# A four-layer graph and expert model on one core: the turn of the expert results, the grouping of the relational stage, and constant matmuls on TensorE

## The chip, the cores and the metric

The kernel runs on one core of one Trainium2 chip. A core has a matrix engine (TensorE, PE in the profile), a vector engine (VectorE, DVE), an activation engine (ScalarE, ACT), a general engine (GpSimd, POOL) and an engine that here only issues transfers (SyncE, SP). Each takes its instructions in the order in which they are written and waits on semaphores that the others raise. The metric is the time of one execution in microseconds on the device. Lower is better.

## What is computed

8192 rows of 128 numbers go through four layers, each added to its input:

```python
x = x + _L0_gnn_ref(_layernorm(x, axis=-1), adj, ...)       # gated graph layer, 3 rounds
x = x + _L0_ffn_ref(_layernorm(x, axis=-1), ...)            # 8 experts, top 2, relu
x = x + _L1_gnn_ref(_layernorm(x, axis=-1), nodemask, adj, ...)   # relational graph layer
x = x + _L1_ffn_ref(_layernorm(x, axis=-1), ...)            # 8 experts, top 2, gelu
```

An expert layer scores each row against 8 experts, takes the best two, and adds their weighted results:

```python
h = gelu(einsum('end,edh->enh', xe, W1) + b1)      # hidden 512; relu in the first expert layer
y = einsum('enh,ehd->end', h, W2) + b2
out = (weights[:, :, None] * sel).sum(axis=1)      # the two chosen experts of each row
```

The relational layer multiplies the rows by a weight, gates them with a sigmoid, and sums them over the neighbours that the adjacency names. A branch for general adjacencies is in the kernel; with the inputs at hand it isn't taken.

## The kernel before, in words

The program has four stages one behind the other, and each ends with results in DRAM that the next one reads: the gated graph layer (to about 470 us), experts 1 (to 806), the relational layer (to 1058), experts 2 (to 1388), and a short last stage that adds the results and stores them. Names that begin with e1 and e2 belong to the expert stages, those with c to the relational stage.

**Experts.** The rows come sorted by expert, in 36 blocks of 512 (NBLK; GT = 4 tiles of 128 rows each). The last 12 blocks consist of two halves of 256 with an expert each. Buffers go round in rings of three (RING), PSUM banks in pairs. A function `rounds` runs `step(b, ...)` on each engine: blocks 0 to 2 written out, 3 to 20 in a loop on the device, 21 to 35 written out. The hidden width of 512 is cut into four pieces, c = 0 to 3 (CH). Each matmul product runs as three passes (lines 205 to 207), since operands are split in a high and a low part of 16 bits.

- PE, in step b, does for each c `up_c(b+1, c)` and `down_c(b, c)`, and behind the four of them `turn(b-1)`: four transposes (line 1547) of the block's results, which wait for `collect(b-1)`.
- ACT, for each c, does `hidden` (line 1586: bias and activation out of PSUM into e1hf) and `hi` (line 1592: the high part into e1hs), with `hi(c)` one place behind `hidden(c+1)`.
- DVE, in step b, does `collect(b-1)` (line 1630: scale and bias of the results into e1yT), in every third step `addresses` (lines 1617 to 1623: where the rows of three blocks go, and with which weight), `share_out(b-2)` (line 1639: the transposed results times their weights into e1ys), and the four `lo(b+1, c)` (line 1605: the low parts into e1hs).
- SP loads the rows of a block transposed (`load`) and their tags (`read_tags`).
- POOL sends each block's e1ys in four indirect transfers to its rows in `results` (line 1511).

**Relational stage.** 16 groups of 512 rows run through 21 steps as a software pipeline; line by line, an engine's step s works on groups s, s-1, s-2 and s-4 at once. On PE: `turn_a` (transposes of the normalised rows c_tok_a, line 1861), `turn_b` (transposes of the rows for the next expert layer, line 1925), `scores` (their eight scores each), `values` (lines 1877 and 205 to 207: four tiles q, in two PSUM banks v), and `neighbours` (line 1890: the sums by adjacency). ACT copies the transposes out of PSUM (`turned_a`, c_xT_a; `turned_b`, c_xT_b). DVE turns scores into S (line 2141) and picks the two best experts for a batch of groups; BATCHES says which. POOL sends rows to their places in `slots` for experts 2 at a rate that `relational_sends` sets for each step. PE's bank TA holds the transposes of turn_a, TBk those of turn_b, RL the sums of neighbours.

## Time and profile before

| | |
|---|---|
| median of three runs | 1425.64 us (1419.89 to 1427.88) |
| profiled execution | 1428.36 us |
| its span | 1426.6 us |
| mean granted TensorE clock | 0.787 |
| PE busy | 918.1 us, 64% |
| DVE busy | 905.9 us, 64% |
| ACT busy | 765.8 us, 54% |
| POOL busy | 733.9 us, 51% |

The profile is of one execution. Its span is what lies between the first and the last recorded instruction; the execution's own time is 1.8 us longer. A share of busy time is a mean over stages that differ, so it has to be read by stage. In the lists an instruction has its start, its duration, its engine and line, what it writes and reads, and in brackets how long the engine stood idle before it and what ended that. Matmuls overlap: one is listed with 0.38 us while the next starts 0.22 us later. The clock stands as a share of full speed, so 0.50 is 1.2 GHz and 1.00 is 2.4 GHz.

### The profile page before, as it was taken

To read this page: it belongs to the slowest core of one execution; us is meant where nothing else is said; L and a number is where in the kernel's file an instruction comes from. 1 tells how busy PE (TensorE), PEld (TensorE's weight loads), DVE (VectorE), ACT (ScalarE), POOL (GpSimd) and SP (SyncE) were. 2 spreads that over 40 slices of the span, in tenths; PEclk is the share of its full clock that TensorE was granted. 3 is DMA by queue.
4 is the path that set the end of the run, shared out by engine and by line. 5 is a ranking of instruction groups with operands and counts; after the bars stand their busy time and mean duration, and the time that the engine had idled before them with its cause. 6 is when DMAs were issued, how large, how long until landed. Compare 5 with 4: busy or idle time off the path is not lost. (4 is left out here: it accounts for less than half of the span.)

```text
span 1426.6 us, 23103 instructions
## 1 busy us (share of the span) xinstructions
PE 918.1 (64%) x5850; PEld 519.1 (36%) x5851; DVE 905.9 (64%) x2456; ACT 765.8 (54%) x1392; POOL 733.9 (51%) x717
## 2 busy tenths in 40 slices
PE   2368778888862357888787176656432968888820
PEld 1244344444432123434565133323210433346620
DVE  5967799999985345555544367767642645554626
ACT  2476767677762145666565165656431655666710
POOL 3501132876757646556544416567566444655540
PEclk9579999999995679899988555555556998999955
DMA  9233221221201524424221223321131342333209
GB/s 249 90 127 94 77 46 23 59 61 48 59 22 42 136 58 100 91 67 85 64 50 45 71 90 119 104 65 55 32 62 52 87 105 58 84 67 70 61 28 340
DMA packets 199164, 115.62 MB, mean 81 GB/s; under 512 B 155084, under 2 KB 175710, under 8 KB 198528
## 3 DMA queue, kind: packets, MB, share of 16 engines
q1 hardware_dynamic: 169008, 69.54, 20.8%
q0 software_dynamic: 17408, 34.13, 7.4%
q10 hardware_dynamic: 12624, 10.49, 2.8%
q8 instruction: 54, 0.88, 0.3%
q14 instruction: 70, 0.57, 0.1%
HBM read 43.80 MB, written 51.61 MB: 67 GB/s over the span
## 5 line engine op out<-in xcount | busy, mean ns | idle before, releaser
L644 POOL DMA_INDIRECT slots<-ROWS,pos x256 | 265.4, 1037 | 78.5 <-issue 71.4
L1511 POOL DMA_INDIRECT results<-e1ys,e1home x144 | 155.5, 1080 | 136.1 <-DVE e1ys L1639 93.7
L1511 POOL DMA_INDIRECT results<-e2ys,e2home x144 | 151.1, 1049 | 136.2 <-DVE e2ys L1639 93.0
L1586 ACT ACTIVATE e1hf<-psum,VT 128x512 f32<-128x512 f32 (+1 forms) x192 | 104.3, 583 | 151.6 <-PE psum L207 82.0
L1605 DVE SCALAR_TENSOR_TENSOR e1hs<-e1hf,e1hs 128x512 f16<-128x512 f32 x144 | 95.6, 690 | 127.4 <-ACT e1hs L1592 88.9
L1586 ACT ACTIVATE e2hf<-psum,VT 128x512 f32<-128x512 f32 (+1 forms) x192 | 104.8, 582 | 126.0 <-remote 59.1
L1605 DVE SCALAR_TENSOR_TENSOR e2hs<-e2hf,e2hs 128x512 f16<-128x512 f32 x144 | 95.8, 691 | 112.5 <-ACT e2hs L1592 83.0
L1363 POOL TENSOR_TENSOR a_Z<-a_Z,a_H 128x512 f32<-128x512 f32 x48 | 68.2, 1420 | 161.5 <-ACT a_Z L1093 159.2
L205 PE MATMUL psum<-e2hs,W 128*128 128x512 f16 (+1 forms) x192 | 66.7, 347 | 55.9 <-DVE e2hs L1605 25.9
L205 PE MATMUL psum<-a_hT,WHH 128*128 128x512 f16 x144 | 58.8, 408 | 52.5 <-ACT a_Z L1093 48.3
L205 PE MATMUL psum<-e1xT,W 128*128 128x512 f16 (+1 forms) x192 | 67.6, 352 | 38.5 <-DMA e1xT<-slots 16.7
L205 PE MATMUL psum<-e1hs,W 128*128 128x512 f16 (+1 forms) x192 | 67.4, 351 | 35.8 <-DVE e1hs L1605 24.9
L1592 ACT ACTIVATE e1hs<-e1hf 128x512 f16<-128x512 f32 x144 | 86.9, 631 | 0.0
L1592 ACT ACTIVATE e2hs<-e2hf 128x512 f16<-128x512 f32 x144 | 86.7, 631 | 0.0
L205 PE MATMUL psum<-e2xT,W 128*128 128x512 f16 (+1 forms) x192 | 66.7, 348 | 23.4 <-issue 11.0
L1804 POOL TENSOR_TENSOR c_rs<-c_var,mhalf 128x12 f32<-128x12 f32 (+2 forms) x22 | 40.5, 1843 | 79.9 <-DVE c_var L2082 45.1
L207 PE MATMUL psum<-e1xT,W 128*128 128x512 f16 (+1 forms) x192 | 67.7, 353 | 3.3 <-issue 3.2
L206 PE MATMUL psum<-e1hs,W 128*128 128x512 f16 (+1 forms) x192 | 67.5, 352 | 2.7 <-issue 1.7
L206 PE MATMUL psum<-e1xT,W 128*128 128x512 f16 (+1 forms) x192 | 67.5, 351 | 2.7 <-issue 2.7
L207 PE MATMUL psum<-e1hs,W 128*128 128x512 f16 (+1 forms) x192 | 67.4, 351 | 2.7 <-issue 2.5
L207 PE MATMUL psum<-e2xT,W 128*128 128x512 f16 (+1 forms) x192 | 66.5, 346 | 1.6 <-issue 1.5
L206 PE MATMUL psum<-e2xT,W 128*128 128x512 f16 (+1 forms) x192 | 66.5, 346 | 0.4 <-issue 0.4
(363 smaller groups left out, 2643.6 us busy)
## 6 DMA issues: line engine op xcount, KB each, us to landing
c_G<-results SPq DMA_DIRECT2D x32, 256.0 KB
d_G<-results SPq DMA_DIRECT2D x32, 256.0 KB, 5.2
slots<-slots SPq DMA_DIRECT2D x16, 264.0 KB
W<-in_L_ffn_W_dram SPq DMA_DIRECT2D x16, 256.0 KB, 3.4
kept<-a_cut SPq DMA_DIRECT2D x16, 256.0 KB, 2.6
slots<-ROWS,pos POOLq DMA_INDIRECT x256
W<-kept SPq DMA_DIRECT2D x8, 512.0 KB
out_dram<-X ACTq DMA_DIRECT2D x16, 256.0 KB, 7.1
```

The costliest lines, as they stand in the source:

```text
L205: pe.matmul(out, lhs(0), rhs(0), start=start, stop=False, skip_group_check=True)
L206: pe.matmul(out, lhs(0), rhs(1), start=False, stop=False, skip_group_check=True)
L207: return pe.matmul(out, lhs(1), rhs(0), start=False, stop=stop, skip_group_check=True)
L644: pool.indirect_dma_start(out=slots, out_offset=bass.IndirectOffsetOnAxis(ap=k["pos"][:, c, t:t + 1], axis=0), in_=k["ROWS32"][:, t, :], i ...
L1363: pool.tensor_tensor(Z[p % 2][:, :], Z[p % 2][:, :], H[p][:, :], ALU.mult).then_inc(zh_sb, 1)
L1511: pool.indirect_dma_start(out=k["results"][m], out_offset=bass.IndirectOffsetOnAxis(ap=home[:, GT * b + q:GT * b + q + 1], axis=0), in_=ys ...
L1586: t = act.activation(hf[c][:, cols], HB[c][:, cols], func, bias=VT[:, bass.ds(e * CH + b1_col + c, 1)], scale=1 / PS)
L1592: act.activation(hs[j][:, 0, c, :], hf[c][:, :], ACT.Copy, scale=AS).then_inc(h_hi, 1)
L1605: dve.scalar_tensor_tensor(out=hs[j][:, 1, c, :], in0=hf[c][:, :], scalar=AS, in1=hs[j][:, 0, c, :], op0=ALU.mult, op1=ALU.subtract).then_ ...
L1804: pool.tensor_tensor(rstd[s % 4][:, lo:hi], var[s % 2][:, lo:hi], k["mhalf"][:, lo:hi], ALU.pow)\
```

## The change

In the expert stages, `turn(b-1)` on PE goes from the end of step b to the place behind `down_c(b, 1)`. On DVE the step shares out block b-1, not b-2, behind `lo(b+1, 1)`; behind the loop only the last block is left to share. `addresses` comes in the second step of three, not the third, and SP reads a block's tags ahead of the next load.

In the relational stage the first two groups form one batch of the selection, so there are 8 batches and not 9, and `relational_sends` starts a step later, with 8. PE does `values` in two halves, the first (v = 0) ahead of `scores`. ACT does `turned_b` ahead of `norms_a` in the first steps. And `stir` multiplies the identity by a constant tile of weights, 256 columns, into banks that are written again before they are read: 40 times at the start, and in each of the 21 steps 6 times ahead of `turn_a`, 5 ahead of `turn_b` and 8 ahead of `neighbours`. Nothing reads these products.

```diff
@@ experts, SP @@
+                if 1 <= b and b + 2 < NBLK:
+                    read_tags(b + 2, rows.pop(b + 2))
                 if b + RING == EARLY:
...
                 if b + RING < NBLK:
                     sp.wait_ge(h_ps, 4 * b + 4)
                     rows[b + RING] = load(b + RING)
-                if 1 <= b and b + 2 < NBLK:
-                    read_tags(b + 2, rows.pop(b + 2))
@@ experts, PE: within the loop over c, and behind it @@
-                if not isinstance(b, int) or b:
-                    turn(b - 1, 1 - v)
+                    if c == 1 and (not isinstance(b, int) or b):
+                        turn(b - 1, 1 - v)
@@ experts, DVE @@
                     collect(b - 1, 1 - v)
-                if j == RING - 1:
+                if j == 1:
                     addresses(b - j, i)
-                if not isinstance(b, int) or b > 1:
-                    share_out(b - 2, (j - 2) % RING, i - (j < 2), v)
                 for c in range(CH):
                     if not last(b):
                         lo(b + 1, (j + 1) % RING, c)
+                    if c == 1 and (not isinstance(b, int) or b):
+                        share_out(b - 1, (j - 1) % RING, i - (j < 1), 1 - v)
...
             collect(end, end % 2)
-            for b in (end - 1, end):
-                share_out(b, b % RING, b // RING, b % 2)
+            share_out(end, end % RING, end // RING, end % 2)
@@ relational stage @@
-BATCHES = [(0, 1), (1, 1)] + [(g, 2) for g in range(2, 16, 2)]
+BATCHES = [(g, 2) for g in range(0, 16, 2)]
...
-    first = ROUTED + 1
+    first = ROUTED + 2
-    wanted = [0 if s < first else (8, 6, 2)[s - first] if s < first + 3 else 8 if s < NG else CARRY for s in range(n)]
+    wanted = [0 if s < first else 8 if s < NG else CARRY for s in range(n)]
...
-            def values(g, p):
+            def values(g, p, v):
                 pe.wait_ge(a_sb, g + 1)
-                for q in range(GT):
-                    v = q // 2
+                for q in range(2 * v, 2 * v + 2):
...
+            def stir(bank, n):
+
+                for i in range(n):
+                    pe.matmul(bank[:, 0:256], ident[:, :], k["WREL"][:, 0, 0, :], start=True, stop=True,
+                              skip_group_check=True)
+
+            stir(TA, 40)
+
             def step(s):
+                stir(TA, 6)
                 if 0 <= s - 1 < NG:
                     turn_a(s - 1, (s - 1) % 2)
+                stir(TBk, 5)
                 if 0 <= s - 4 < NG:
                     turn_b(s - 4)
+                if 0 <= s - 1 < NG:
+                    values(s - 1, (s - 1) % 2, 0)
                 if 0 <= s - 4 < NG:
                     scores(s - 4)
                 if 0 <= s - 1 < NG:
-                    values(s - 1, (s - 1) % 2)
+                    values(s - 1, (s - 1) % 2, 1)
                 if 0 <= s - 2 < NG:
+                    wait_from(pe, rel_sb, s - 3)
+                    stir(RL[s % 2], 8)
                     neighbours(s - 2, s % 2)
@@ relational stage, ACT @@
                     turned_a(s - 1, (s - 1) % 2)
+                if 0 <= s - 4 < NG:
+                    turned_b(s - 4)
                 if s < SPLIT:
                     norms_a(s, s % 2)
-                if 0 <= s - 4 < NG:
-                    turned_b(s - 4)
```

How this stands in the engines' rows is shown at three places. On PE, in step 2 of experts 1, the four transposes of turn (identf and e1yT into PSUM) change place; one piece of the difference, with the part between left out by the list itself (the matmuls of up 2, down 2, up 3 and down 3):

```order
@@ -1388,4 +1388,5 @@
 L1450 TENSOR_LOAD owner
 L1450 ISA x2
+L1547 MATMUL psum<-identf,e1yT 128x128 x4
 L205 ISA
 L205 MATMUL psum<-e1xT,W 128x512
@@ -1408,5 +1409,4 @@
 L207 REGISTER_ALU
 L207 MATMUL psum<-e1hs,W 128x512
-L1547 MATMUL psum<-identf,e1yT 128x128 x4
 L1426 UNCONDITIONAL_BRANCH
 L1426 ISA
```

The turn moved ahead of the second half of the step's matmuls. On DVE, steps 1 and 2 of experts 1, before (e1hs is lo, e1yT collect, the four e1chosen to e1share are addresses, e1ys is share_out):

```order
L1605 SCALAR_TENSOR_TENSOR e1hs<-e1hf,e1hs 128x512 x4
L1450 TENSOR_LOAD owner
L1450 ISA x2
L1630 ISA
L1630 TENSOR_SCALAR e1yT<-psum,VT 128x512
L1617 TENSOR_TENSOR e1chosen<-e1label,owned 128x12
L1619 TENSOR_TENSOR e1part<-e1chosen,e1label 128x12
L1620 SCALAR_TENSOR_TENSOR e1home<-e1chosen,e1label 128x12
L1623 TENSOR_TENSOR e1share<-e1part,e1label 128x12
L1639 TENSOR_TENSOR e1ys<-psum,e1share 128x512
L1605 SCALAR_TENSOR_TENSOR e1hs<-e1hf,e1hs 128x512 x4
```

and after, the end of step 1 and step 2:

```order
L1605 SCALAR_TENSOR_TENSOR e1hs<-e1hf,e1hs 128x512 x2
L1639 TENSOR_TENSOR e1ys<-psum,e1share 128x512
L1605 SCALAR_TENSOR_TENSOR e1hs<-e1hf,e1hs 128x512 x2
L1450 TENSOR_LOAD owner
L1450 ISA x2
L1630 ISA
L1630 TENSOR_SCALAR e1yT<-psum,VT 128x512
L1605 SCALAR_TENSOR_TENSOR e1hs<-e1hf,e1hs 128x512 x2
L1639 TENSOR_TENSOR e1ys<-psum,e1share 128x512
L1605 SCALAR_TENSOR_TENSOR e1hs<-e1hf,e1hs 128x512 x2
```

The share of a block now follows its own collect, with two of the four lo ahead of it and two behind, where it stood behind the collect of the block after it. On PE in a step of the relational stage, before, the scores (WGATE) stand right behind the transposes of turn_a and turn_b:

```order
L1861 MATMUL psum<-ident,c_tok_a 128x128 x8
L1925 MATMUL psum<-ident,ROWS 128x128 x8
L205 MATMUL psum<-WGATE,c_xT_b 128x8
L206 MATMUL psum<-WGATE,c_xT_b 128x8
L207 MATMUL psum<-WGATE,c_xT_b 128x8
```

and after, with the first half of values (relbias, WREL and c_xT_a) and five matmuls of stir (WREL and ident):

```order
L1860 MATMUL psum<-ident,c_tok_a 128x128 x8
L1938 MATMUL psum<-WREL,ident 128x256 x5
L1923 MATMUL psum<-ident,ROWS 128x128 x8
L1875 MATMUL psum<-relbias,ones 128x256 x2
L205 MATMUL psum<-WREL,c_xT_a 128x256
L206 MATMUL psum<-WREL,c_xT_a 128x256
L207 MATMUL psum<-WREL,c_xT_a 128x256
L1875 MATMUL psum<-relbias,ones 128x256 x2
L205 MATMUL psum<-WREL,c_xT_a 128x256
L206 MATMUL psum<-WREL,c_xT_a 128x256
L207 MATMUL psum<-WREL,c_xT_a 128x256
L205 MATMUL psum<-WGATE,c_xT_b 128x8
```

The ten matmuls of the first two q of values moved ahead of the scores, and the matmuls of stir are new.

## Rows read from the trace of the kernel before

**Rows 1.** By stage: length, busy time (instructions) by engine, PEclk, DMA share, GB/s.

```profile
500.00:791.00 291.00, 225.36 (x1254) 128.33 (x1254) 152.18 (x273) 167.87 (x325) 154.88 (x144) 0.88 0.32 69
...
806.00:1058.00 252.00, 138.92 (x985) 76.45 (x985) 169.83 (x783) 132.64 (x274) 142.17 (x157) 0.51 0.25 78
...
1100.00:1373.00 273.00, 220.33 (x1255) 127.25 (x1252) 147.81 (x270) 167.05 (x323) 141.28 (x134) 0.91 0.32 71
```

**Rows 2.** Timeline, PE, experts 2: start, us, engine, line, out<-in, count.

```profile
1135.61 0.38 PE L207 MATMUL psum<-e2xT,W 128*128 128x512 f16 x1
...
1139.29 0.38 PE L207 MATMUL psum<-e2hs,W 128*128 128x512 f16 x1
...
1141.23 0.38 PE L207 MATMUL psum<-e2xT,W 128*128 128x512 f16 x1
...
1142.09 0.60 PE L1547 MATMUL psum<-identf,e2yT 128*128 128x128 f32 x4
```

**Rows 3.** The same stretch on ACT and DVE.

```profile
1136.71 1.14 ACT L1592 ACTIVATE e2hs<-e2hf 128x512 f16<-128x512 f32 x2
...
1138.79 0.75 DVE L1630 TENSOR_SCALAR e2yT<-psum,VT 128x512 f32<-128x512 f32 x1
```

**Rows 4.** Timeline, half blocks of experts 1, PE and DVE.

```profile
770.13 0.42 PE L207 MATMUL psum<-e1xT,W 128*128 128x256 f16 x1
...
774.18 0.88 DVE L1630 TENSOR_SCALAR e1yT<-psum,VT 128x256 f32<-128x256 f32 x2 [0.81 <-issue]
```

**Rows 5.** Timeline, first and last of the 66 steps counted, PE and DVE.

```profile
530.97 0.38 PE L207 MATMUL psum<-e1hs,W 128*128 128x512 f16 x1
...
534.85 0.75 DVE L1630 TENSOR_SCALAR e1yT<-psum,VT 128x512 f32<-128x512 f32 x1
...
1364.73 0.42 PE L207 MATMUL psum<-e2hs,W 128*128 128x256 f16 x1
...
1367.82 0.88 DVE L1630 TENSOR_SCALAR e2yT<-psum,VT 128x256 f32<-128x256 f32 x2 [0.69 <-issue]
```

**Rows 6.** Timeline, POOL, ends of both expert stages.

```profile
789.11 0.98 POOL L1511 DMA_INDIRECT results<-e1ys,e1home  x1 [7.76 <-DVE e1ys L1639]
...
803.28 0.98 POOL L1511 DMA_INDIRECT results<-e1ys,e1home  x1 [0.30 <-issue]
...
1370.80 0.98 POOL L1511 DMA_INDIRECT results<-e2ys,e2home  x1 [7.49 <-DVE e2ys L1639]
```

**Rows 7.** Relational stage, one step: ACT, PE; then DVE grouped by line.

```profile
885.75 1.02 ACT L1993 ACTIVATE c_xT_a<-psum 128x1024 f16<-128x1024 f16 x1 [0.96 <-PE psum L1861]
887.99 1.02 ACT L2006 ACTIVATE c_xT_b<-psum 128x1024 f16<-128x1024 f16 x1 [1.22 <-remote]
...
889.07 0.19 PE L205 MATMUL psum<-WGATE,c_xT_b 128*128 128x8 f16 x1 [3.42 <-ACT c_xT_b L2006]
...
889.49 0.60 PE L1877 MATMUL psum<-relbias,ones 1*128 1x256 f16 x2
...
892.06 0.60 PE L1877 MATMUL psum<-relbias,ones 1*128 1x256 f16 x2
...
L2141 DVE TENSOR_TENSOR S<-psum,c_rs 128x32 f32<-128x32 f32 x16 | 3.0, 188 | 21.7 <-PE psum L207 21.7
```

**Rows 8.** Relational stage: windows with the clock, and PE in them.

```profile
996.80:999.70 2.90, 2.81 (x27) 2.52 (x24) 1.92 (x7) 1.50 (x5) 2.29 (x3) 0.50 0.18 60
999.70:1003.40 3.70, 1.24 (x18) 0.78 (x19) 1.75 (x12) 2.41 (x3) 3.08 (x4) 0.96 0.13 42
1003.40:1007.00 3.60, 3.60 (x15) 1.10 (x14) 2.57 (x13) 0.00 (x0) 3.10 (x3) 0.50 0.08 28
...
1002.99 0.27 PE L206 MATMUL psum<-WREL,c_xT_a 128*128 128x256 f16 x1
1003.10 0.27 PE L207 MATMUL psum<-WREL,c_xT_a 128*128 128x256 f16 x1
```

**Rows 9.** Relational stage, DVE by line: an operation of the selection.

```profile
L582 DVE TENSOR_TENSOR v_wide<-S,v_top 128x64 f32<-128x64 f32 (+1 forms) x9 | 2.0, 221 | 0.3
```

## The prediction

> **What bounds the kernel now.** I read the table of busy time by stage first [rows 1], then the order of time on each engine inside one step. In the two expert stages TensorE (PE) is the bound: 225.36 of 291 us and 220.33 of 273 us busy, at a granted clock of 0.88 and 0.91, while DVE is busy for about half of the time. The relational stage is another matter: at a clock of 0.51 (the 1.2 GHz level) PE is busy for 139 of 252 us and DVE for 170, so there waits between engines set the pace.
>
> A step of an expert stage that runs without a pause is on PE an unbroken row of 24 matmuls and 4 transposes [rows 2]: the last matmul of up_c(b+1, 3) starts at 1135.61 and again at 1141.23, a period of 5.62 us. The transposes of turn(b-1) stand last in the step (1142.09). Beside it runs the chain that I take for the main thing in this change [rows 3]: after up_c of c=3, at 1135.61, ACT does hidden(3) and two hi (1136.71 to 1137.85), DVE two lo and collect, which ends at 1138.79 + 0.75 = 1139.54. That is 3.93 us after the start of the matmul that released it. No engine waits for collect now: the turn that needs it comes 2.55 us later.
>
> **Experts, the turn.** The change puts turn(b-1) right behind the matmuls of down_c(b, 1), whose last starts at 1139.29; the next could start at 1139.51. So even in a smooth step collect's end and the slot of the turn meet within 0.03 us. This has a consequence: turn, up_c(b+1, 2), down_c(b, 2) and up_c(b+1, 3) then all stand behind collect(b-1), and collect(b) stands behind up_c(b+1, 3). The loop closes: 3.93 (chain) + about 0.1 (PE starts on a signal) + 0.44 (turn: 0.60 for its four transposes, less the 0.16 by which the next matmul starts before the end of the last) + 0.65 + 0.65 (up 2, down 2) + 0.43 (up 3 to its last start) = 6.20 us, against the 5.62 that PE's own work takes. That is +0.58 us for a smooth step. The half blocks at the end have a longer chain (770.13 to 774.18 + 0.88, 4.93 us [rows 4]), so their loop is about 7.2 us.
>
> Most steps aren't smooth: 33 steps of experts 1 lie 7.8 us apart on average, of experts 2 7.6; 11 and 10 of the periods are under 5.75. For each step b = 3 to 35 of both stages I took the lateness: collect's end less the slot behind the last matmul of down_c(b, 1) (its start + 0.22). The first is 535.60 - 531.19 = 4.41 us, and the last 1368.70 - 1364.95 = 3.75 [rows 5]. Over 33 steps the positive ones add up to 52.8 us in experts 1 (31 of 33 are late) and 47.2 in experts 2 (29 of 33). The smooth steps hold 6.4 and 3.8 of it, the steps with a pause 46.3 and 43.4. Their true price lies between nothing (PE waits again later in such a step anyway, and the new wait only takes that one's place) and all of it. I take half: ACT, not PE, is what pauses there, and what PE loses before up_c(b+1, 2) reaches ACT's next input only when ACT is back at work. So experts 1: 11 x 0.58 + 23.2 = 29.6 us; experts 2: 10 x 0.58 + 21.7 = 27.5. Sum **+57 us**, with bounds 12 (smooth steps alone) and 102 (12 + 46.3 + 43.4).
>
> On DVE, share_out(b-1) now waits for that turn between lo(b+1, 1) and lo(b+1, 2). Queued behind it are two lo; their hidden needs up_c(b+1, 2), which PE issues behind the same turn, so DVE has the 0.68 us of the share to spare: nothing. On SP read_tags(b+2) passes ahead of load(b+3), and it waits for addresses, which come one step sooner too; one load of three is held back by about half a step in both orders, and a load is issued two steps before its use: nothing. Addresses (four operations of DVE, under 0.2 us each) only change place.
>
> **Experts, the end.** POOL starts the sends of the last three blocks at 789.11 after 7.76 us without work, and the twelfth starts at 803.28 [rows 6], so one each 1.29 us; experts 2 look the same from 1370.80 on (7.49 idle). The next stage fetches only behind them. With shares a step sooner, block 33's four go in the idle time, and eight are left from about 788.5 on, so the last starts near 797.5: 6 us sooner. Bounds 0 and 7.5. Two stages: **-12**.
>
> **Relational stage.** The sends of this stage are 16 by s = 7 in both kernels, and turned_b changes place with norms_a only in steps 4 and 5: nothing. The rest depends on the clock.
> Half of values moves ahead of scores. At 1.2 GHz it takes 892.06 - 889.49 = 2.57 us [rows 7]. It fills a wait of 3.42 us for c_xT_b, but it can start only when c_xT_a is done (886.77), and c_xT_b is done 2.24 us later (889.01): scores come 0.33 later here, 0 to 1.8 in the 16 steps, about 0.6 in the mean, 10 us in sum. Behind scores waits DVE, S at L2141, the largest wait of DVE in the stage (21.7 us). What values gain is worth little: PE then waits longer for c_tok_a.
> The dummy matmuls (stir), 19 in a step, cost what a 256-column matmul takes: 0.11 us at 2.4 GHz (1002.99 to 1003.10, [rows 8]), so 0.21 at 1.2. The 8 ahead of neighbours lie off the path; the 6 and 5 ahead of the transposes are on it where the input is there already: 11 x 0.21 = 2.3 us a step at 1.2 GHz, of which I put 1.4 in pauses: 0.95 x 16 = 15 us. One batch less in the selection saves DVE some 15 operations of 0.22 us, 3.3 us [rows 9].
> Never at 2.4 GHz, then: 10 + 15 - 3 = +22. At 2.4 throughout: half of values takes some 1.3 us by the two levels (an estimate) and delays nothing; stir, with half of 11 x 0.11 hidden, +10; the batch -3; and PE's work ahead of scores takes half its time, of which DVE can get back at most its 21.7 us of waits at L2141, and I put 14: 10 - 3 - 14 = -7. Which of them it will be is told by [rows 8]: from 999.7, behind 8 matmuls of neighbours and 16 transposes without a pause, the clock stood at 0.96, and 3.7 us later, after another wait for c_xT_b, at 0.50. Stir fills waits of PE, but not that one, which values take. I take the middle: **+7.5**, bounds -7 and +22.
> The Trainium skill, "TensorE: Matmul & The Clock Gate" (Part 4, PE-mode transpose), says that the high clock does not engage for transposes, which don't count as PE-busy in the same way. The trace disagrees as far as it goes, since the rise came behind 8 matmuls and 16 transposes. By the page only stir and values would lift the clock, and the sum would take +22 in place of +7.5, the case A below.
>
> **Sum.** 1428.36 (the profiled execution; span 1426.6) + 57 - 12 + 7.5 = 1480.9. It was 2.7 above the median of 1425.64, so against the median: **1478 us**.
>
> **Rivals.**
> A. The clock stays low in the relational stage: +22, so 1493. For it: the wait behind c_xT_a remains. Against it: stir stands in the pauses ahead of both transposes.
> B. The other side. The turn's wait falls wholly into pauses that PE has in such steps anyway (the steps with a pause are two thirds of all), so only the smooth steps pay, and the relational stage comes out at its best: 12 - 12 - 7 = -7, so 1419; with collect ready in time in the smooth steps as well, 1407. It decides where the turns of both stages cost below about 10 us, 0.15 a step. Against it: in a stalled step the pause comes ahead of down_c(b, 1), and the new wait is added behind it.
> C. The whole lateness is paid in each step: 102 - 12 + 7.5, so 1523. Against it: ACT's pauses swallow part.
> D. The pauses swallow the turn's wait, but the relational stage costs 7.5: 12 - 12 + 7.5, so 1433, the same within 0.5%. In this case the change doesn't do what it says either: shares come sooner and nobody needs them but the last eight sends.
>
> **How the numbers follow.** Forecast 0.56 (1455 to 1505), A 0.15, B 0.13, C 0.08, D 0.08. A measurement of this kernel tells about 0.5% (7 us) from no change; below 1418.5 is faster, above 1432.8 slower. B's chance goes to faster but for a little, 0.12; same takes that little and most of D, 0.09; slower 0.79. The range 1425 to 1513 leaves out most of B and C, 2 in 10.
>
> **What would show it.** In the profile after: the row of the turn's first matmul gets an idle time released by DVE e1yT (collect), some 0.1 us in smooth steps and 1 to 3 in others; smooth steps lie 6.2 us apart, not 5.62; the expert stages are about 30 us longer up to the last turn; POOL sends eight or fewer behind the last but one share; the relational stage is between 245 and 275 us with a clock above 0.51. If smooth steps stay at 5.62, the chain is shorter than I read it, and I am wrong on the main term; if the pauses of ACT shrink by as much as PE waits, B or D holds.

## The result, and the profile after

The changed kernel takes 1450.26 us in the median of six runs (1446.14 to 1455.27), the kernel before 1429.69 in the six beside them. The ratio is 1.0198, with a 95% interval of 1.0146 to 1.0251. The forecast was 1478 us: the direction is right and the time lies in the range of 1425 to 1513, but below the 1455 at which the forecast's own case begins. The loss is 20.6 us by the medians, where 52 were forecast. The profiled execution took 1450.58 us (span 1448.4), 22.2 us more than that of before. Some executions of a kernel are disturbed and take longer, and every ratio in this text compares undisturbed ones only, so it can differ from the ratio of the medians.

By stage, first as in [rows 1] (columns as there):

```profile
500.00:791.00 291.00, 221.15 (x1256) 128.42 (x1255) 152.82 (x280) 171.40 (x327) 162.83 (x148) 0.91 0.31 69
...
804.00:1088.00 284.00, 187.07 (x1380) 113.50 (x1381) 167.44 (x764) 132.38 (x272) 139.55 (x157) 0.67 0.22 69
...
1130.00:1396.00 266.00, 215.36 (x1229) 126.54 (x1230) 144.82 (x266) 169.15 (x323) 144.37 (x135) 0.92 0.33 74
```

The clock of the relational stage is up from 0.51 to 0.67, and the stage is over 30 us longer. The two expert stages are no longer than they were. Three lengths, each from the start of one instruction to the start of another in the timelines, show it best; each is from the one profiled execution of its kernel. An expert stage is taken from PE's first matmul on e1xT or e2xT to POOL's last send, the relational stage from the first row that DVE adds (X<-X,c_G) to the first matmul of experts 2:

| kernel | experts 1 | relational | experts 2 |
|---|---|---|---|
| before | 326.1 | 252.8 | 322.0 |
| after | 322.2 | 285.5 | 314.1 |
| difference | -3.9 | +32.7 | -7.9 |

Together +20.9; 1.6 more come ahead of the experts (first matmul at 478.8, not 477.2). The sum of the prediction was +45 for the experts and +7.5 for the relational stage. So both of its parts were wrong, in opposite directions.

**The turn's loop closed as worked out.** A step of the changed kernel on PE, and collect on DVE (start, us, engine, line, names, count, idle before):

```profile
606.16 0.38 PE L205 MATMUL psum<-e1xT,W 128*128 128x512 f16 x1
...
608.53 0.38 PE L207 MATMUL psum<-e1hs,W 128*128 128x512 f16 x1
609.29 0.66 PE L1547 MATMUL psum<-identf,e1yT 128*128 128x128 f32 x4 [0.39 <-DVE e1yT L1630]
...
612.38 0.38 PE L205 MATMUL psum<-e1xT,W 128*128 128x512 f16 x1
...
608.49 0.75 DVE L1630 TENSOR_SCALAR e1yT<-psum,VT 128x512 f32<-128x512 f32 x1
```

The last matmul of down c=1 starts at 608.53, collect ends at 609.24, the turn starts 0.05 later behind a wait that the trace puts down to it, and the next step begins at 612.38: a period of 6.22 us; in the 32 periods of experts 1 from step 3 on there is none under 6.19, where [rows 2] showed 5.62.

**It cost nothing, because PE only stood in another place.** From step 3 to step 35, experts 1 take 248.9 us (534.51 to 783.44) and took 249.0 (528.59 to 777.57). In these two stretches, by line (busy, mean ns, idle before and what ended that), before:

```profile
L1586 ACT ACTIVATE e1hf<-psum,VT 128x256 f32<-128x256 f32 (+1 forms) x172 | 91.7, 576 | 93.6 <-PE psum L207 44.4 <-remote 39.9 <-DVE e1hs L1605 7.1
...
L205 PE MATMUL psum<-e1xT,W 128*128 128x256 f16 (+1 forms) x176 | 59.8, 339 | 11.5 <-issue 7.3 <-ACT e1hf L1586 3.5 <-DMA e1xT<-slots 0.6
...
L205 PE MATMUL psum<-e1hs,W 128*128 128x256 f16 (+1 forms) x173 | 59.2, 342 | 19.5 <-DVE e1hs L1605 15.4 <-issue 3.9
...
L1547 PE MATMUL psum<-identf,e1yT 128*128 128x128 f32 x130 | 20.5, 278 | 3.2 <-issue 3.1
```

and after:

```profile
L1586 ACT ACTIVATE e1hf<-psum,VT 128x256 f32<-128x256 f32 (+1 forms) x175 | 93.3, 571 | 92.3 <-PE psum L207 73.9 <-issue 10.2 <-DVE e1hs L1605 7.5
...
L205 PE MATMUL psum<-e1hs,W 128*128 128x256 f16 (+1 forms) x172 | 58.3, 339 | 5.0 <-DVE e1hs L1605 4.2 <-issue 0.7
...
L1547 PE MATMUL psum<-identf,e1yT 128*128 128x128 f32 x128 | 22.6, 303 | 41.6 <-DVE e1yT L1630 27.8 <-issue 13.8
```

PE stood for 43.7 us in all before, most of it ahead of the products (the two rows of L205 here, and 9.4 us in those of L206 and L207) and 3.2 ahead of the turn (L1547). After, it stands for 47.1, and 41.6 of it ahead of the turn. ACT's idle time ahead of hidden is the same, 93.6 and 92.3 us. What changed there is the label: before, 39.9 us in 10 waits end with nothing that the trace knows ("remote"), after there is no such row, and the row put down to PE has grown from 44.4 to 73.9. So a row "remote" that is gone is not yet a pause that is gone. Experts 2 have the same: PE stands for 43.5 us before, 0.5 of it ahead of the turn, and for 40.3 after, 34.0 of it there; ACT for 90.0 and 85.3.

**The ends** came as forecast, a little smaller. POOL, the end of experts 1, to be read against [rows 6]:

```profile
786.46 1.33 POOL L1511 DMA_INDIRECT results<-e1ys,e1home  x1 [4.21 <-DVE e1ys L1639]
...
800.97 0.98 POOL L1511 DMA_INDIRECT results<-e1ys,e1home  x1 [0.30 <-issue]
```

POOL was without work for 4.21 us, not 7.76, and its last send starts 8.5 us behind the start of the last share (800.97 against 792.5; before 803.28 against 790.73, 12.5 us).

**The relational stage** got two longer waits on DVE. By line, X before and then X and S after:

```profile
L2077 DVE TENSOR_TENSOR X<-X,c_rl 128x512 f32<-128x512 f32 x16 | 11.0, 690 | 6.0 <-issue 5.1 <-ACT c_rl L1958 0.8
...
L2089 DVE TENSOR_TENSOR X<-X,c_rl 128x512 f32<-128x512 f32 x16 | 11.0, 688 | 25.4 <-ACT c_rl L1970 21.1 <-issue 4.3
...
L2153 DVE TENSOR_TENSOR S<-psum,c_rs 128x32 f32<-128x32 f32 x16 | 3.1, 191 | 38.5 <-PE psum L207 38.5
```

X, which adds the neighbours' sums that ACT has taken out of PSUM (c_rl), waits for 25.4 us where it waited for 6.0. S at L2153 is L2141 of [rows 7]: its wait has gone from 21.7 to 38.5 us. PE by line, after:

```profile
L1938 PE MATMUL psum<-WREL,ident 128*128 128x256 f16 x396 | 73.0, 344 | 12.3 <-PEq L160 11.9 <-issue 0.4
L1875 PE MATMUL psum<-relbias,ones 1*128 1x256 f16 x128 | 35.9, 378 | 39.0 <-DVE c_sg L2081 32.6 <-ACT c_xT_a L2005 6.4
...
L1888 PE MATMUL psum<-c_vs,MASK 128*128 128x128 f16 x128 | 14.4, 282 | 5.8 <-DVE c_vs L2103 5.4 <-issue 0.4
L1860 PE MATMUL psum<-ident,c_tok_a 128*128 128x128 f16 x128 | 11.8, 242 | 18.7 <-DVE c_tok_a L240 14.0 <-issue 4.6
L205 PE MATMUL psum<-WGATE,c_xT_b 128*128 128x8 f16 x64 | 7.1, 176 | 3.3 <-ACT c_xT_b L2018 3.3
```

and before:

```profile
L1877 PE MATMUL psum<-relbias,ones 1*128 1x256 f16 x128 | 38.2, 399 | 4.9 <-DVE c_sg L2069 2.6 <-ACT c_xT_a L1993 2.2
...
L1890 PE MATMUL psum<-c_vs,MASK 128*128 128x128 f16 x128 | 16.9, 313 | 8.5 <-DVE c_vs L2091 8.5
...
L1861 PE MATMUL psum<-ident,c_tok_a 128*128 128x128 f16 x128 | 16.5, 310 | 45.2 <-DVE c_tok_a L240 40.5 <-issue 4.7
```

Values (L1875, before L1877) wait for 39.0 us where they waited for 4.9, and 32.6 of these end with DVE's c_sg, the gating of the group before. The row of constant matmuls (L1938) is busy for 73 us.

### The profile page after: what moved, and what is told of

Same layout as the page of the kernel before. It is cut to its first block and busy times, and to the rows that moved or that the text cites. A ratio compares the mean times of both kernels' runs of the same rounds, so it can differ in the third digit from the quotient of the medians.

```text
span 1448.4 us, 23892 instructions
## 1 busy us (share of the span) xinstructions
PE 964.5 (67%) x6248; PEld 559.7 (39%) x6249; DVE 901.9 (62%) x2437; ACT 770.0 (53%) x1390; POOL 739.6 (51%) x717
## 5 line engine op out<-in xcount | busy, mean ns | idle before, releaser
L1511 POOL DMA_INDIRECT results<-e1ys,e1home x144 | 160.7, 1116 | 127.3 <-DVE e1ys L1639 84.0
L1511 POOL DMA_INDIRECT results<-e2ys,e2home x144 | 154.0, 1069 | 124.5 <-DVE e2ys L1639 78.4
L205 PE MATMUL psum<-a_hT,WHH 128*128 128x512 f16 x144 | 59.7, 414 | 52.0 <-ACT a_Z L1093 48.6
L205 PE MATMUL psum<-e1xT,W 128*128 128x512 f16 (+1 forms) x192 | 67.3, 351 | 26.0 <-DMA e1xT<-slots 16.1
L205 PE MATMUL psum<-e2hs,W 128*128 128x512 f16 (+1 forms) x192 | 66.5, 346 | 24.4 <-DVE e2hs L1605 24.3
L1938 PE MATMUL psum<-WREL,ident 128*128 128x256 f16 x399 | 73.6, 345 | 12.3 <-PEq L160 11.9
L205 PE MATMUL psum<-e1hs,W 128*128 128x512 f16 (+1 forms) x192 | 66.0, 344 | 22.5 <-remote 11.6
L205 PE MATMUL psum<-e2xT,W 128*128 128x512 f16 (+1 forms) x192 | 66.8, 348 | 5.3 <-DMA e2xT<-slots 4.6
L207 PE MATMUL psum<-e1xT,W 128*128 128x512 f16 (+1 forms) x192 | 66.9, 348 | 0.8 <-issue 0.8
L207 PE MATMUL psum<-e2xT,W 128*128 128x512 f16 (+1 forms) x192 | 66.4, 346 | 0.8 <-issue 0.8
L206 PE MATMUL psum<-e1xT,W 128*128 128x512 f16 (+1 forms) x192 | 66.9, 348 | 0.0
L206 PE MATMUL psum<-e2hs,W 128*128 128x512 f16 (+1 forms) x192 | 66.5, 346 | 0.0
L206 PE MATMUL psum<-e2xT,W 128*128 128x512 f16 (+1 forms) x192 | 66.4, 346 | 0.0
```

Of the source, the lines that this page charges most:

```text
L205: pe.matmul(out, lhs(0), rhs(0), start=start, stop=False, skip_group_check=True)
L206: pe.matmul(out, lhs(0), rhs(1), start=False, stop=False, skip_group_check=True)
L207: return pe.matmul(out, lhs(1), rhs(0), start=False, stop=stop, skip_group_check=True)
L1511: pool.indirect_dma_start(out=k["results"][m], out_offset=bass.IndirectOffsetOnAxis(ap=home[:, GT * b + q:GT * b + q + 1], axis=0), in_=ys ...
L1938: pe.matmul(bank[:, 0:256], ident[:, :], k["WREL"][:, 0, 0, :], start=True, stop=True, skip_group_check=True)
```

## The experiments

Theory 1 is the forecast. Theory 2, formed on the trace above: the expert part costs nothing or gains, and the relational part costs some 32 us. For the relational stage the rivals are the constant matmuls and the values ahead of scores.

The runs of the kernel before spread from 1406.34 to 1454.03 us over the study. Its relational stage, in the five traces that run it unchanged, spreads from 243.8 to 252.8 us, so the lengths of stages are the steadier measure there.

### The two parts alone

The kernel `e_only` has the hunks of the expert stages and nothing else; `r_only` has those of the relational stage.

> The expert part of the change alone (turn, share_out, addresses and read_tags moved), with the relational stage of before. Theory 1, the forecast: the turn costs 57 us and the ends of the stages give back 12, so about +45 us against the kernel before. Theory 2, from the trace of the changed kernel, where the 33 steps b = 3 to 35 take 248.9 us against 249.0 in experts 1 and ACT's long unexplained pauses (39.9 us in 10 waits) are gone: the wait for collect takes the place of these pauses, the steps cost nothing, and only the ends show: 5 to 15 us faster than before.

Measured: 1416.98 us in the median of ten runs (1411.84 to 1428.03), before 1434.32; ratio 0.9969 (0.9916 to 1.0022). Stages: 323.4, 243.8, 316.4. The waits of experts 1, steps 3 to 35 (251.7 us):

```profile
PE psum L1547 <- DVE e1yT L1630: 27.6, 20, 5.8
...
PE psum L1547 <- issue: 12.6, 11, 2.9
...
ACT e1hf L1586 <- remote: 1.7, 1, 1.7
```

Theory 1's +45 us is excluded. The part is at least not slower, and PE stands ahead of the turn as in the changed kernel, while the row "remote" of ACT is all but gone. A gain of 17 us, which the medians show, is not shown by the ratio.

> The relational part of the change alone (pairs, sends, values in halves, turned_b ahead of norms_a, stir), with the expert stages of before. Theory 1, the forecast: +7.5 us, at most +22. Theory 2: from the first row that the stage adds to the first matmul of experts 2 the changed kernel takes 32 us longer, so +27 to +36 us alone.

Measured: 1457.6 us (1453.6 to 1464.85), ratio 1.0252 (1.0134 to 1.037). The relational stage takes 284.0 us. The time is 23 us longer by the medians and some 36 by the ratio, the stage 31 us longer than the 252.8 of before. Theory 2 holds: the whole loss is here.

### Why the turn cost nothing

```diff
-                    if c == 1 and (not isinstance(b, int) or b):
+                    if c == 2 and (not isinstance(b, int) or b):
                         turn(b - 1, 1 - v)
```

> As e_only, but the turn stands behind down_c(b, 2) and share_out behind lo(b+1, 2), one piece later. The loop from up_c(b+1, 3) over collect to the turn and back then leaves out turn, up 2 and down 2, and is shorter than PE's own 5.62 us. Both theories expect smooth steps of 5.62 us again in place of 6.20. If PE's loop of 6.20 has a price, this kernel is 8 to 20 us faster than e_only. If pauses of ACT take up what the turn leaves, the steps b = 3 to 35 stay at 243 to 250 us a stage, ACT's pauses come back, and the time is that of e_only within 4 us.

Measured: 1438.24 us (1434.55 to 1442.72), ratio 1.0122 (1.0002 to 1.0241), so slower than e_only. The smooth steps are back at 5.62 us, 8 and 9 of them a stage, but steps 3 to 35 take 253.3 and 266.1 us. Waits in experts 1, steps 3 to 35, columns as above:

```profile
ACT e1hf L1586 <- remote: 17.6, 8, 4.8
...
PE psum L1547 <- DVE e1yT L1630: 11.1, 12, 3.0
```

The row "remote" is back in part (17.6 us, and 33.6 in experts 2), with PE's waits for collect between those of before and after. Both cases of the expectation fail: a price of PE's loop would have made this kernel faster than e_only, and theory 2 said the time would be the same. It is 21 us longer, and the profiled execution has it in experts 2 alone (338.9 us against 316.4; experts 1 take 323.0 and 323.4). Why is open.

```diff
                 wait_from(pe, y_sb, b - 1)
+                for n in range(3):
+                    pe.matmul(YB[v][:, :], W1[:, 0, 0:P], W1[:, 0, 0:BLK], start=True, stop=True, ...)
                 for q in range(GT):
                     t = pe.transpose(YB[v][:, q * P:(q + 1) * P], ...)
```

> The kernel before, with the turn at its old place and three matmuls of 512 columns on a constant tile ahead of the four transposes in each expert step: PE works 3 x 0.215 = 0.65 us longer, so a smooth step takes 6.26 us and not 5.62, as in the changed kernel, but nothing waits for collect. Theory 1 (each step pays): 10 to 12 smooth steps a stage and part of the others, 13 to 40 us slower than before. Theory 2 (pauses of ACT fill what PE leaves): the steps b = 3 to 35 stay at 243 to 253 us, ACT's pauses without a releaser in the trace fall from about 40 us a stage to under 15, and the time is that of before within 8 us. Rival: the pauses go because of the new wait itself, then they stay here at about 40 us and the steps take 260 us or more.

Measured: 1391.04 to 1437.01 us, median 1414.55, ratio 0.9878 (0.949 to 1.0265): nothing can be told of the time, except that no run shows the 13 to 40 us. The profiled execution was the longest of the four. ACT's waits labelled "remote" in it, experts 1 and 2:

```profile
ACT e1hf L1589 <- remote: 59.4, 15, 7.1
...
ACT e2hf L1589 <- remote: 26.5, 7, 8.9
```

Steps 3 to 35 take 264.3 and 244.9 us. A slower PE alone doesn't end these waits, so theory 2 fails on them. The rival, that it is the new wait that does, is left, though experts 2 don't take the 260 us that it names.

```diff
+                pe.wait_ge(yT_ps, b + 1)
                 if not isinstance(b, int) or b:
                     turn(b - 1, 1 - v)
```

> The kernel before, with one wait more on PE in each expert step: ahead of the turn, which stays at the end of the step, PE waits for its own last matmul of down_c(b, 3). PE then stands for some 0.3 us a step, as it does in the changed kernel where it waits for collect, and nothing else moves. Theory 2a: the pauses of ACT without a releaser, some 40 us a stage, are signals of PE that arrive 4 to 6 us behind the record of their matmul when PE runs on without a wait, and a wait on PE in each step ends them: they fall under 15 us a stage, and the steps b = 3 to 35 take 215 to 235 us in place of 245 to 250, so 20 to 60 us faster than before. Theory 2b: what pauses is set by something else (ACT, DVE, the transfers), and the wait for collect only took the pauses' place: the steps take 243 to 260 us and the time is that of before or up to 10 us more.

Measured: 1456.6 us (1440.4 to 1466.66), ratio 1.0172 (1.0003 to 1.034). Theory 2a falls in its time and in ACT's waits, which don't go. Theory 2b is not met either: steps 3 to 35 take 253.8 us in experts 1 but 275.4 in experts 2, and the time is 24.5 us above the median of before (1432.06), not up to 10. What the run shows is where such waits come from (waits in experts 1):

```profile
PE psum L1547 <- remote: 35.9, 8, 7.4
ACT e1hf L1587 <- remote: 35.8, 12, 9.6
```

One of the eight in full: the collect that the turn also needs, PE's last matmul of down_c(b, 3), ACT's hidden, and the turn:

```profile
607.16 0.75 DVE L1631 TENSOR_SCALAR e1yT<-psum,VT 128x512 f32<-128x512 f32 x1
...
610.38 0.38 PE L207 MATMUL psum<-e1hs,W 128*128 128x512 f16 x1
...
614.68 0.69 ACT L1587 ACTIVATE e1hf<-psum,VT 128x512 f32<-128x512 f32 x1 [5.44 <-remote]
...
616.10 1.11 PE L1547 MATMUL psum<-identf,e1yT 128*128 128x128 f32 x4 [5.35 <-remote]
```

PE, which waits here for a signal of its own last matmul, stands for 35.9 us in 8 waits of 1.7 to 7.4 us. The turn waits for collect as well, but collect had ended 3.0 to 10.3 us before the turn began in all eight, so it did not hold it. So the signal arrived long behind the record of its matmul, and ACT, which waits in the same stretch for a signal of PE too, shows the same. These waits have a period: in both stages PE has one in step b = 12, 15, 18, 21 and 24 (3.2 to 5.4 us each). Among the half blocks of experts 2, with more matmuls in a step, two lie two steps apart (b = 29 and 31, 5.7 and 5.2 us), which a ring of three buffers would not give. What has this period no run shows.

The kernels side by side, experts 1 from step 3 to step 35. "Behind the record" is the part of ACT's idle time ahead of hidden that lies behind the record of the very matmul that it needs (the n-th hidden with the n-th up_c, and behind the lo that frees its buffer), in waits of over 0.5 us:

| kernel | length, us | PE idle | of it ahead of the turn | ACT idle ahead of hidden | behind the record |
|---|---|---|---|---|---|
| before | 249.0 | 43.7 | 3.2 | 93.6 | 84.8 in 29 |
| after | 248.9 | 47.1 | 41.6 | 92.3 | 31.2 in 19 |
| e_only | 251.7 | 47.8 | 40.3 | 93.4 | 32.3 in 19 |
| turn2 | 253.3 | 46.7 | 12.6 | 99.2 | 72.3 in 29 |
| pace | 264.3 | 41.4 | 3.4 | 109.0 | 93.5 in 30 |
| drain | 253.8 | 49.4 | 38.1 | 98.6 | 61.6 in 32 |

PE stands for 41 to 49 us in all six, wherever the wait is put.

### What costs the relational stage its time

```diff
-                if 0 <= s - 4 < NG:
-                    scores(s - 4)
-                if 0 <= s - 1 < NG:
-                    values(s - 1, (s - 1) % 2)
+                if 0 <= s - 1 < NG:
+                    values(s - 1, (s - 1) % 2, 0)
+                if 0 <= s - 4 < NG:
+                    scores(s - 4)
+                if 0 <= s - 1 < NG:
+                    values(s - 1, (s - 1) % 2, 1)
```

This alone is `vsplit_only`; with pairs, sends and the order on ACT it is `r_nostir`, the relational part without stir.

> The relational part without the constant matmuls, expert stages of before. If the constant matmuls are what costs 30 us (PE has 399 of them, 73 us busy), this is within 8 us of the kernel before. If it is the half of values ahead of the scores, which now wait for DVE's gating of the group before, it is 20 to 35 us slower than before, and nothing or a few us away from the relational part with them; if the raised clock helped, it is slower than that part.

Measured: 1451.83 us (1433.76 to 1460.54), ratio 1.0178 (1.0017 to 1.0339); relational stage 269.7 us. That is 20 us above the unchanged ones and 14 below r_only, so neither case holds alone: values ahead of scores cost, and so do the constant matmuls.

> Values in two halves, the first ahead of scores, and nothing else. The length that counts is the relational stage, from the first row that DVE adds to the first matmul of experts 2: 252.9 us before, 269.7 with the whole relational part but stir. If the half of values ahead of the scores is the cost without stir (DVE waits for S behind PE's 2.6 us of values, which wait for DVE's gating), 12 to 20 us longer than before. Rival: the pairs and the sends that begin a step later cost it, then this one is within 5 us of before.

Measured: 1460.63 us (two runs, 1456.21 and 1465.05); relational stage 271.1 us. DVE and PE by line:

```profile
L2142 DVE TENSOR_TENSOR S<-psum,c_rs 128x32 f32<-128x32 f32 x16 | 3.1, 191 | 43.8 <-PE psum L207 43.8
```

```profile
L1876 PE MATMUL psum<-relbias,ones 1*128 1x256 f16 x128 | 38.3, 400 | 36.0 <-DVE c_sg L2070 24.9 <-ACT c_xT_a L1994 11.2
```

The same two waits as after, with no constant matmul in the kernel: values wait for c_sg (24.9 us) and for c_xT_a (11.2), scores stand behind them, and DVE waits for scores for 43.8 us, not 21.7.

> Groups in pairs from the start, the sends that go with them, turned_b ahead of norms_a in the first steps, and nothing else. By the theory that values cost the time, the relational stage is 0 to 6 us shorter than 252.9 (one batch of selection less, 3.3 us). By the rival it is 10 to 17 us longer.

Measured: 1440.32 us (two runs; the expert stages took 339.0 and 322.7 in the profiled one); relational stage 246.2 us. Nothing shows that pairs cost; whether they gain 3 us can't be told.

For the constant matmuls, all 19 a step (`stir_only`), only the 8 ahead of neighbours (`stir8`), and only the 6 and 5 ahead of the transposes (`stir11`), each on the kernel before:

> The constant matmuls alone, on the kernel before. The relational part with them took 284.0 us, without them 269.7. If their cost is their own time ahead of the transposes, the stage is 8 to 18 us longer than 252.9 at a clock of 0.6 to 0.7. If they only cost through the values that stand behind them on PE, less than 5. If the raised clock pays without the values in front of the scores, it is shorter than before.

Measured: 1464.13 us (two runs); relational stage 269.8 us, its row with the clock (last but two):

```profile
815.00:1083.00 268.00, 187.31 (x1382) 113.19 (x1380) 169.53 (x784) 133.18 (x274) 141.06 (x138) 0.70 0.23 73
```

> Of the constant matmuls only the 8 ahead of neighbours in each step, on the kernel before. By the prediction these lie off the path: the relational stage is within 5 us of the 244 to 253 us that it takes without them. If what costs is PE's longer row of work, wherever it stands (stir alone: 269.8 us), it is 257 to 265 us.

Measured: 1441.92 us (two runs); relational stage 265.5 us:

```profile
800.00:1070.00 270.00, 154.33 (x1090) 87.97 (x1091) 165.78 (x762) 131.72 (x271) 145.87 (x161) 0.59 0.23 72
```

On PE the neighbours' sums and the ranking of the chosen experts stand behind these 8. What DVE does with them, X and v_wide, waits longer; v_wide first before, then both in stir8:

```profile
L630 DVE TENSOR_TENSOR v_wide<-psum,base 128x64 f32<-128x64 f32 (+1 forms) x9 | 1.9, 214 | 10.9 <-remote 7.6 <-PE psum L620 3.3
...
L2089 DVE TENSOR_TENSOR X<-X,c_rl 128x512 f32<-128x512 f32 x16 | 11.0, 688 | 11.8 <-issue 6.0 <-ACT c_rl L1970 5.8
...
L630 DVE TENSOR_TENSOR v_wide<-psum,base 128x64 f32<-128x64 f32 (+1 forms) x9 | 1.9, 216 | 19.2 <-remote 15.2 <-PE psum L620 4.0
```

X waits for 11.8 us (6.0 before), v_wide for 19.2 (10.9), while S waits for 19.1, no longer than before.

> Of the constant matmuls only those ahead of the transposes, 6 and 5 in each step, and the 40 at the start, on the kernel before. The prediction put the whole price here: 2.3 us a step, 0.95 of it on the path, so the relational stage 8 to 15 us longer than the 244 to 253 us without them. By the run with the 8 alone (265.5 us, against 269.8 with all 19) the 8 carry it, and this one is within 6 us of the stage without them.

Measured: 1427.88 us (eight runs, 1415.87 to 1433.48), ratio 1.0061 (0.9976 to 1.0147); relational stage 258.6 us:

```profile
814.00:1069.00 255.00, 170.23 (x1247) 100.14 (x1246) 168.98 (x782) 132.67 (x274) 140.98 (x118) 0.65 0.24 76
```

The kernels with two runs have no clear ratio, so the argument on this stage rests on its length in one trace each. Side by side; five kernels run the stage without a change, which shows how far it varies by itself:

| kernel | relational stage, us |
|---|---|
| before, e_only, turn2, pace, drain (unchanged) | 252.8, 243.8, 250.3, 249.9, 250.3; mean 249.4 |
| pairs alone (pairs_only, and best1 below) | 246.2, 251.3 |
| values in halves alone; with pairs | 271.1; 269.7 |
| stir ahead of the transposes; ahead of neighbours; both | 258.6; 265.5; 269.8 |
| whole relational part (r_only, after) | 284.0, 285.5 |

### The best of both

`best1` has the expert part with pairs, sends and the order on ACT, without values in halves and stir.

> The expert part of the change, with pairs, sends and turned_b ahead of norms_a from the relational part, without values in halves and without the constant matmuls. By the single runs: the expert part alone 1417 us in the median, the pairs 0 to 6 us less. So 1405 to 1420 us, 10 to 28 below the medians of before (1430 to 1434 in the last runs). If pairs cost what they seemed to in their own run (1440 us, where the expert stages took 339 and 323 us), 1420 to 1430.

Measured: 1419.92 us (ten runs, 1414.68 to 1429.92), ratio 0.9986 (0.9939 to 1.0033). Stages 319.2, 251.3, 319.5. By the medians it beats the changed kernel by 30 us; against the kernel before only the medians (1432.06) differ, and the ratio shows no change. The pairs add nothing to e_only that can be told.

## Why the prediction was right in sign and wrong in its parts

**The turn in smooth steps.** The loop of 6.20 us was right to 0.02. That it would cost 0.58 for each smooth step was not: e_only has the same 6.2 and is not slower, and the mean distance of the steps is 7.8 us in experts 1 both before and after.

**The turn in steps with a pause.** The step that failed is "I take half". The price was nothing, the lower bound that the prediction itself names: PE stands elsewhere in the same steps anyway, and the new wait takes that wait's place (43.7 us of idle time before, 47.1 after, of which 3.2 and 41.6 ahead of the turn). Over the three kernels with the turn behind c=1 (after, e_only, best1) experts 1 take 321.6 us in the mean and experts 2 316.7; over the eight with the experts of before (before, r_only, r_nostir, vsplit_only, pairs_only, stir_only, stir8, stir11) 329.6 and 325.9. The two stages together take 636 to 640 us in the three and 648 to 663 in the eight. So by the traces the whole expert part is worth -17 us, not +45, though no ratio confirms a gain (0.9969 for e_only, 0.9986 for best1). Behind the last share POOL's sends give 4 to 6 of it a stage; where the rest comes from is not shown. For the expert stages this is the mechanism of rivals B and D: the new wait falls into waits that PE has anyway. What would show it by the prediction's own words, that ACT's pauses shrink by as much as PE waits, is not what the rows show: ACT stands as long as before.

What is shown: PE stands as long as before, in another place; and signals of PE can come 1.7 to 7.4 us behind the record of their matmul (drain). Where PE waits for collect in every step (after, e_only, best1), less of ACT's idle time lies behind PE's record, 30 to 32 us in experts 1 in place of 84.8; where it seldom waits (turn2), 72.3. A slower PE doesn't lower this (pace, 93.5), a wait of PE for itself lowers it to 61.6 (drain). Why the signals come late stays open, and so does whether they come sooner with the wait for collect or PE's record only runs less far ahead of them. One pause of before, PE and then ACT, shows how it hides in the trace:

```profile
619.47 0.38 PE L207 MATMUL psum<-e1xT,W 128*128 128x512 f16 x1
...
623.79 0.38 PE L207 MATMUL psum<-e1xT,W 128*128 128x512 f16 x1
...
618.94 0.69 ACT L1586 ACTIVATE e1hf<-psum,VT 128x512 f32<-128x512 f32 x1 [0.26 <-DVE e1hs L1605]
624.13 0.69 ACT L1586 ACTIVATE e1hf<-psum,VT 128x512 f32<-128x512 f32 x1 [4.50 <-PE psum L207]
...
629.84 0.69 ACT L1586 ACTIVATE e1hf<-psum,VT 128x512 f32<-128x512 f32 x1 [4.50 <-remote]
```

The matmul that hidden(1) waits for is on record from 619.47 to 619.85, and ACT starts at 624.13. The trace names PE as what ended this wait, but the record of the matmul that hidden(1) needs had ended 4.28 us before; so a row with PE as its releaser can be the same kind of wait as one labelled "remote". The trace also holds the instants at which the signals arrive: the matmuls of up_c on record to 621.15, 622.44, 624.17 and 627.64 are signalled at 629.64, 629.74, 629.90 and 629.97. PE needs 1.3 us for the six matmuls from one of them to the next, so it did not run them between these signals: the signals were held up, not the work. The prediction read these rows as pauses of ACT and built the price on PE's records; the records are not the time at which PE's results can be used.

**The ends.** Forecast -12; the sends behind the last share give -4.0 and -4.0 in the changed kernel, -6.1 and -5.1 in e_only (12.5 and 12.0 before; 8.5 and 8.0 after; 6.4 and 6.9). Right in kind; -8 in the changed kernel is two thirds of the forecast.

**The relational stage.** Forecast +7.5 with bounds of -7 and +22; measured +33, and r_only lies 35 above the mean of the unchanged ones. Beyond the bound, by two terms:

- Values ahead of scores: 10 forecast, 21.7 measured (271.1 - 249.4). I priced only the wait for c_xT_a. The bank into which the first half writes is freed by DVE's gating of the group before (c_sg), and that stands late in DVE's step, right ahead of S. So the chain in each step became gating, half of values (2.57 us), scores, S, all one behind the other, where scores did not depend on the gating before. In the order it was there to see: "wait_from(pe, val_sb, ...)" stands in the function that moved.
- The 8 of stir ahead of neighbours: 0 forecast ("off the path"), 16 measured. [rows 7] show one step; the row of L1890 above shows the stage: neighbours waited for c_vs for only 8.5 us in all 16 steps, so 8 x 0.21 us in each step in front of them (27 us in 16 steps at 1.2 GHz, an estimate) had little cover. In stir8 the price shows on DVE at what stands behind neighbours (X and v_wide). Of v_wide's 19.2 us 15.2 end with "remote", so late signals of PE may be part of the price; no run separates the two. The 11 ahead of the transposes: 10 to 15 forecast, 9 measured, though this one lies only 5.8 us above the longest unchanged stage.
- The batch less: -3 forecast, -3 and +2 measured, not to be told from nothing.

The prices don't add: 21.7 + 16 + 9 is 47, and the whole costs 35. With values in halves already there, all 19 constant matmuls cost 14 us (284.0 - 269.7), alone 20.

**The clock** rose, as the middle case assumed: to 0.67 in the changed kernel and 0.70 with stir alone. But it bought nothing that the stage could use: with stir alone S waited for 23.5 us, not less than the 21.7 of before, and the stage got longer. The error was to let "2.4 GHz" stand for a gain of 14 us at S, when scores came to stand behind something else. On the rule weighed in the prediction: the Trainium skill ("TensorE: Matmul & The Clock Gate", Part 4, PE-mode transpose) says that transposes don't engage the high clock. The prediction saw [rows 8] against it; but there matmuls and transposes ran together, so the row speaks neither for nor against it. Here constant matmuls ahead of the transposes lifted the stage from 0.51 to 0.65 (stir11), which agrees with the page as far as it goes; no run has transposes alone to test it. By the page stir would have lifted the clock, as it did, so the page was no ground for case A. Case A, in which the clock stays low, is excluded by the rows, and its +22 for the stage would have been too little as well.

**The sum.** -17 and +35 make +18, near the 20.6 measured. That the range held is luck: a term too large by 62 and one too small by 28 partly cancelled.

## What to carry to other kernels

Before a new wait is priced by lateness, add up how long the waiting engine stands in the same steps already: the new wait may only move that time, and half of the lateness is not a price. Before a wait is said to be gone, add up all rows of the engine's idle time, whatever releaser each row names. When work moves ahead of other work on an engine, take over all of its waits, the one for its output buffer among them, and ask who now stands behind that release. Work that fills pauses is free only where a row of waits shows the pause, and a higher clock is worth only what waits for that engine.

## What the runs showed of the hardware

TensorE's signals can come several us behind the record of the matmul that raises them: in drain PE waits for its own last matmul 8 times for 35.9 us in all, 1.7 to 7.4 us each. In the kernel before, waits of ACT that lie over 0.5 us behind the record of the matmul they need add up to 84.8 us in experts 1 and 79.4 in experts 2. Its 13 runs beside e_only spread over 40 us (1412.58 to 1453.05), the 10 of e_only over 16 (1411.84 to 1428.03); that late signals are the reason is not shown. In the relational stage waits without a releaser are more with the constant matmuls: 38.4 to 47.9 us in 16 to 20 waits (stir11, stir8, r_only, after, stir_only), against 15.9 to 33.5 in 8 to 14 in the kernels without them.

The raised clock did not pay for the matmuls that raised it: with 19 constant matmuls a step the stage's granted clock went from 0.51 to 0.70, and the stage from 249.4 us in the mean to 269.8.
